# One layer of gated linear attention and an expert-choice FFN on one core: another order of the head's loads, stores, sums, transposes and gather

## What is computed

```
q, k = silu(xn Wq'), silu(xn Wk');  v = xn Wv';  log_f = log_sigmoid(xn Wf' + delta)
lf = cumsum(log_f) inside chunks of 128 tokens, 16 heads of 16 features
o  = (q exp(lf)) S  +  (q k' * exp(lf_i - lf_j), i >= j) v
S  = exp(tot) S + (k exp(tot - lf))' v                       # from chunk to chunk
s  = (o * rsqrt(mean(o*o)) * norm_weight) Wo'

affinity = softmax(xn gate_w');  per expert (8) the 128 tokens of each batch with the highest affinity
out[idx] += gating * ((silu(xi w_gate') * (xi w_up')) w_down')
x + s * silu(out)
```

## Time and profile before

| | us |
|---|---|
| median of 3 runs | 902.36 |
| lowest and highest | 902.20 and 903.24 |
| the profiled execution | 906.21 |
| its span in the trace | 904.5 |

### The profile page before, as it was taken

One profiled execution on the slowest core, in us unless ns is written; L12 is line 12 of the kernel. 1 busy time (PEld: TensorE's weight loads), 2 busy tenths in 40 slices (PEclk: granted clock), 3 DMA queues, 4 the chain that ended last, 5 costly groups with the idle time before them and its releaser, 6 DMA issues.

```text
span 904.5 us, 15830 instructions
## 1 busy us (share of the span) xinstructions
PE 799.0 (88%) x5648; PEld 681.6 (75%) x5648; DVE 570.1 (63%) x1034; ACT 498.4 (55%) x1165; POOL 427.5 (47%) x383
## 2 busy tenths in 40 slices
PE   1654389999999999999999999999999999999930
PEld 1443378888888888888888888888888888888820
DVE  5676256556755676557655775567656755656585
ACT  4653565566546664566556655765566545653421
POOL 5645561357426662556165815563356425561120
PEclk9965699999999999999999999999999999999965
DMA  8829798776766685769587777776776757754827
GB/s 280 283 102 196 181 256 296 170 165 146 219 145 164 159 214 148 161 158 199 168 190 167 141 226 155 173 158 189 172 147 180 199 145 210 167 111 160 248 80 223
DMA packets 132847, 163.89 MB, mean 181 GB/s; under 512 B 11808, under 2 KB 102432, under 8 KB 132640
## 3 DMA queue, kind: packets, MB, share of 16 engines
q1 hardware_dynamic: 119904, 145.00, 58.1%
q0 software_dynamic: 12288, 16.79, 11.9%
q10 hardware_dynamic: 576, 1.09, 0.3%
HBM read 117.48 MB, written 45.35 MB: 180 GB/s over the span
## 4 chain that ended last, share of the span: by engine, by line
PE 72%; DVE 7%; DMA 5%; ACT 3%; issue 3%; POOL 3%; SPq 1%; DVEq 0%; ACTq 0%; POOLq 0%
PE g_ps L1415 17%; PE up_ps L1415 16%; PE y_ps L1441 16%; PE m_ps L1333 5%; PE a_ps L1381 4%; PE o_ps L1405 4%; PE m_ps L1341 3%; PE m_ps L1363 2%; DMA w_raw<-w_experts 2%; PE m_ps L1358 1%; POOL w_r L794 1%; PE o_ps L1397 1%; ACT dec_both L963 1%; DVE sg L1284 1%; DMA w_r<-ffn_dram 1%
## 5 line engine op out<-in xcount | busy, mean ns | idle before, releaser
L1441 PE MATMUL y_ps<-w_r,hid_r 128*128 128x256 f32 x1536 | 206.2, 284 | 5.2 <-DVE hid_r L1298 5.2
L1415 PE MATMUL up_ps<-xgt,w_r 128*128 128x512 f32 x768 | 204.8, 402 | 0.0
L1415 PE MATMUL g_ps<-xgt,w_r 128*128 128x512 f32 x768 | 202.0, 398 | 2.5 <-DVE sg L1284 2.5
L1441 PEld LDWEIGHTS y_ps<-w_r,hid_r 128*128 128x128 f32 x1536 | 194.2, 191 | 6.4 <-DVE hid_r L1298 5.6
L1284 DVE SCALAR_TENSOR_TENSOR sg<-sg,g_ps 128x512 f32<-128x512 f32 x128 | 87.5, 684 | 166.6 <-ACT sg L1054 166.6
L794 POOL TENSOR_TENSOR w_r<-w_raw,w_r 128x768 fp32r<-128x768 f32 x64 | 122.2, 1909 | 95.5 <-ACT w_r L983 95.3
L1415 PEld LDWEIGHTS up_ps<-xgt,w_r 128*128 128x128 f32 x768 | 139.2, 190 | 25.9
L1415 PEld LDWEIGHTS g_ps<-xgt,w_r 128*128 128x128 f32 x768 | 135.6, 189 | 25.9 <-DVE sg L1284 2.9
L1054 ACT ACTIVATE sg<-g_ps 128x512 f32<-128x512 f32 x128 | 76.4, 597 | 124.1 <-PE g_ps L1415 124.1
L824 POOL DMA_INDIRECT ffn_dram<-y_sb,idx_all x64 | 103.2, 1612 | 83.6 <-DVE y_sb L1206 67.9
L789 POOL TENSOR_SCALAR_AFFINE_SELECT lb_row<-lb_row 128x1024 f32<-128x1024 f32 x64 | 78.1, 1230 | 104.6 <-DMA lb_row<-lb_tiles 104.5
(11 more groups left out here) (239 smaller groups left out, 944.4 us busy)
## 6 DMA issues: line engine op xcount, KB each, us to landing
lb_row<-lb_tiles SPq DMA_DIRECT2D x64, 512.0 KB, 4.7
w_raw<-w_experts SPq DMA_DIRECT2D x64, 384.0 KB, 3.6
qk_dram<-qk_r SPq DMA_DIRECT2D x32, 512.0 KB, 4.3
k_st<-qk_dram SPq DMA_DIRECT2D x96, 128.0 KB, 4.2
arena<-qk_dram SPq DMA_DIRECT2D x192, 64.0 KB, 4.3
x_all<-x SPq DMA_DIRECT2D x8, 512.0 KB, 10.3
xn_dram<-xn SPq DMA_DIRECT2D x8, 512.0 KB, 4.8
e_row<-lb_tiles SPq DMA_DIRECT2D x64, 64.0 KB
```

The costliest lines, as they stand in the source:

```text
L1415: mm = pe.matmul(bank[:, :], w_r[:, m, a, at:at + P], xgt[:, b, k, half * 512:(half + 1) * 512], start=(j == 0 and k == 0), stop=(j == len ...
L1441: mm = pe.matmul(y_ps[:, j, :], hid_r[p][:, a, j * P:(j + 1) * P], w_r[:, m, b, DOWN:DOWN + D], start=(m == 0 and q == 0 and j % 2 == 0), ...
```

## The change

Nothing is computed in another way. Instructions are put in another place in the order, and the second gate chain gets other tiles:

- **TensorE:** the affinities are turned after the first job in place of the third; `sums_turned(0)` goes ahead of job v; `sums(1)` goes from ahead of job "top" to behind it.
- **ScalarE:** Ln of the first gate part goes behind the fourth job's Tanh, with the third job's high part ahead of it; the fourth job's high part goes ahead of `sums(0)`; job v's copy goes behind `gates_left(0)`.
- **GpSimd:** low part 2 goes ahead of `gates_log(0)`; the first gather goes ahead of `gates_left(1)`, and waits for one store of the block before (xt_stored) in place of the second chain's end.
- **VectorE:** (TOP_STEPS takes the place of 3 * ROUNDS in every wait on topk) the last replacement of the search is left out; nothing read its result.
- **SyncE:** the keys of the first stack are loaded once the key stores have landed (`load_keys`), both query stores go ahead of `store_lb(0)`, and the first stack's queries ahead of `load_lb`. In the loop `load_rows` goes from step 2 of a batch's 16 to step 6.
- **Tiles:** `spare[1]` uses y_sb, th and small, and xg no longer.

```diff
@@ tiles
-                 [t[:, n:n + 384] for n in (0, 384) for t in (y_sb[:, :, :].rearrange("p t d -> p (t d)"),
-                                                              xg[:, :, :].rearrange("p t d -> p (t d)"))]]
+                 [y_sb[:, 0:2, :].rearrange("p t d -> p (t d)")[:, 0:384], th[:, 0:384],
+                  y_sb[:, 2:4, :].rearrange("p t d -> p (t d)")[:, 0:384], small[:, 512:896]]]
@@ SyncE
+                def load_keys(ch):
+                    b, s, cols = ch // TPB, ch % 2, slice(ch % TPB * P, (ch % TPB + 1) * P)
+                    for g in range(3):
+                        rows = qk_dram[b % 2, K, K_PART[g], :, cols].rearrange("(r p) n -> p r n", p=PAIR)
+                        sp.dma_start(f32(k_st[s][PAIR * g:PAIR * (g + 1), :, :]), rows).then_inc(st_in[s], 16)
                 def load_stacks(ch):
...
+                    if ch >= 1:
+                        load_keys(ch)
                     for g in range(3):
-                        rows = qk_dram[b % 2, K, K_PART[g], :, cols].rearrange("(r p) n -> p r n", p=PAIR)
-                        sp.dma_start(f32(k_st[s][PAIR * g:PAIR * (g + 1), :, :]), rows).then_inc(st_in[s], 16)
...
                 for i in range(2):
                     store_part(0, i)
-                store_lb(0)
+                for n in range(2):
+                    sp.wait_ge(qk_out[n], 16)
+                load_keys(0)
                 for i in range(2, 4):
                     store_part(0, i)
+                store_lb(0)
+                load_stacks(0)
                 sp.wait_ge(d_out, 16)
                 sp.wait_ge(chain, CHAIN)
                 for n in range(2):
                     load_lb(n)
-                load_stacks(0)
                 load_rows(0)
                 load_stacks(1)
...
-                    if at == 2 and b + 1 < B:
-                        if b >= 1:
-                            load_x(b + 1)
+                    if at == 2 and b >= 1 and b + 1 < B:
+                        load_x(b + 1)
+                    if at == 6 and b + 1 < B:
                         load_rows(b + 1)
@@ GpSimd
+    TOP_STEPS = 3 * ROUNDS - 1
...
                 def gather(e, half):
-                    pool.wait_ge(topk, 3 * ROUNDS + 2)
+                    pool.wait_ge(topk, TOP_STEPS + 2)
                     if e == 0 and half == 0:
-                        pool.wait_ge(chain, 2 * CHAIN)
+                        pool.wait_ge(xt_stored[0], 16)
...
                 low_part(1)
+                low_part(2)
                 gates_log(0)
-                low_part(2)
...
                     if u == 0:
+                        gather(0, 0)
                         gates_left(1)
-                    if u == 1:
-                        gather(0, 0)
@@ ScalarE
                 evacuate(FIRST[2])
-                gates_ln(0)
                 split(FIRST[2])
                 evacuate(FIRST[3])
+                gates_ln(0)
+                split(FIRST[3])
                 sums(0)
-                split(FIRST[3])
                 sums_turned(0)
+                gates_left(0)
                 evacuate(FIRST[4])
-                gates_left(0)
@@ TensorE
-                for job in FIRST[:3]:
-                    make(job)
+                make(FIRST[0])
                 pe.wait_ge(soft, 5)
                 for c in range(2):
                     mm = pe.transpose(aff_ps[:, c * P:(c + 1) * P], kd[:, c * P:(c + 1) * P], ident[:, :])
                 mm.then_inc(aff_turned, 1)
-                make(FIRST[3])
+                for job in FIRST[1:4]:
+                    make(job)
                 sums(0)
+                sums_turned(0)
                 make(FIRST[4])
-                sums_turned(0)
...
-                    if u == 0:
-                        sums(1)
                     if u == 1:
                         sums_turned(1)
                     if 1 <= n <= XS:
                         down(n - 1)
                     if second:
                         make(second)
+                    if u == 0:
+                        sums(1)
```

More of the change, by code:

```diff
@@ L836, in gates_sum @@
                     if p == 1:
-                        pool.wait_ge(xt_stored[0], 16)
+                        pool.wait_ge(xt_stored[1], 16)
                     shape = [P, PART[p].stop - PART[p].start, H]
@@ L957, in decays @@
                     if t == 3:
-                        act.wait_ge(topk, 3 * ROUNDS + 1)
+                        act.wait_ge(topk, TOP_STEPS + 1)
                     if t >= 4:
@@ L1201, in gated @@
                         dve.wait_ge(zeroed, 16 * B)
-                        dve.wait_ge(topk, 3 * ROUNDS + 2)
+                        dve.wait_ge(topk, TOP_STEPS + 2)
                     dve.wait_ge(scattered, 16 * TPB * n)
@@ L1245, in search @@
                 def search(first, rounds):
-                    for n in range(3 * first, 3 * (first + rounds)):
+                    for n in range(3 * first, min(3 * (first + rounds), TOP_STEPS)):
                         top_step(dve, topk, n, aff_t, top_val, top_at)
@@ L1271, in _ @@
                     evacuate(job)
-                dve.wait_ge(topk, 3 * ROUNDS)
+                dve.wait_ge(topk, TOP_STEPS)
                 low, high = slice(0, B * E), slice(B * E, 2 * B * E)
@@ L1367, in make @@
                     elif kind == "top":
-                        pe.wait_ge(topk, 3 * ROUNDS + 1)
+                        pe.wait_ge(topk, TOP_STEPS + 1)
                         pe.transpose(m_ps[:, 0:P], top_rev[:, :], ident[:, :])
```

## The result

The change is faster: 896.95 us (median of four runs, 895.99 to 897.55) against 902.70 us for the kernel before on the same chip. The ratio is 0.9942, with a 95% interval of 0.9922 to 0.9962, that is 3.4 to 7.0 us. The medians differ by 5.75 us, where 8.0 was forecast. The predicted 894.4 is 2.6 us too low; the range of 890.0 to 899.5 holds the time. The profiled execution of the change took 896.94 us, its own median, with a span of 895.2 us. That of the kernel before was 3.5 us above its median, so the two profiles differ by 9.3 us and the medians by 5.75. In the second set of runs one execution of the change (1164 us) and one of the kernel before (1042 us) ran at a lower clock, and the ratios leave them out.

What follows compares the result with a forecast made beforehand. The head was taken to bound the gain, set by three weight loads in a row and SyncE's queue. Terms 4.5 + 3.3 + 1.5 - 1.3 = 8.0 us took the median from 902.36 to 894.4; range 890 to 899.5.

Steps and rivals of the forecast that it cites:

- rival (d): Solid stretch: moved row loads make weight loads land 2.6 us late six times; net +7.6, time 910; chance 0.06.
- Rival (a): Head: query stores land in 4.3 us, so queries are late; gain 5.2, time 897.2; chance 0.12.
- Rival (b): Head's end: moved row loads block weight blocks 6 and 7, landing after 11.0 us; time 897.9; chance 0.13.
- (c): Head: weight blocks 2 and 4 land in 3.5 us instead of 5.3; gain 11, time 891.4; chance 0.15.
- part 4: SyncE's moved row loads: weights leave at 92.05, 7.85 us earlier; block 7 taken at 120.1, 8.0 us earlier.
- Part 1: Prologue's early sums, stores and keys: search some 4 us earlier, lb_row no gain, second chain still ends at 76.5.
- Part 2: TensorE's second sums start at 76.7 (3.4 us earlier), top transposes leave the path (1.1 us): job v 4.5 us earlier.
- Part 3: GpSimd's first gather goes at about 78 instead of 87.13, costed at nothing.
- that cover: GpSimd's last gates step, behind the gather's 5 us, ends near 84, needed only after 86; losing this slack costs up to 2 us.
- The term for landings: Head's weight loads: blocks 2 and 4 land in 5.3 us instead of 6.82 (1.5 us gained); block 6 takes 6.82.
- 3.3 + 1.5 - 1.3 = 3.5: Moved row loads: 3.3 us of SyncE queue order, 1.5 of shorter landing, less 1.3 for rows ahead of block 6.
- The 4.5 for the prologue and the gather: Head up to job v: sums 3.4 us earlier plus 1.1 for the top transposes, with the gather costed at nothing.

Runs made afterwards that it cites:

- the second set of runs: The changed kernel unaltered, run again with a second profile, against the kernel before: ratio 0.9947 (0.9927 to 0.9967).
- both repaired: The change with mask(1) held until VectorE's four copies are through and the first gather back in step 1: 895.03 us, ratio 0.9923 to the kernel before.

## Why the prediction was right, and where it was off

**The start and the end of the head.** That only the head moves was right: the solid stretch is unchanged (687.54 busy of 690 against 687.60), which refutes rival (d). Block 7 was forecast at 120.1 and came at 120.73 and 119.27. Rival (a) didn't come: TensorE waited 1.6 us for the queries, long before it had the search's result. By the time alone 896.95 can't be told from that rival's 897.2; only the marks in the profile part them. Rival (b) would have block 7 at 121.5 and more; (c) had it at 117.1.

**The step that was off: the profiled execution carried over to the median.** The prediction took 8.0 us from the one profiled execution and set the result 3.85 below it, as if that excess lay outside the head. In the second profile of before most of it is gone, and it had lain in the head: 4.5 us of span are missing, 3.55 of these already at block 7, 1.2 by the earlier sums and most of the rest by the landings of the weights. From that profile's 124.57 to the forecast 120.1 are 4.5 us, and to the measured 119.27 to 120.73 they are 3.8 to 5.3; the medians differ by 5.75 and, in the second set of runs, by 4.8 (902.34 times 0.0053). The forecast place was good, partly by luck (part 4), and the place that it was subtracted from was a late one. The forecast span of 896.5 was within 1.5 us of both profiles of the change (895.2 and 895.0).

**Part 1** was nearly right in its marks: affinities at 47.99 (forecast 48.0), the copies at 73.97 (74.5), first lb_row issued at 66.03 (66.9). mask 0 came at 71.25, not 72.5, so its transfer wasn't the fixed end that the prediction made of it (by its own sign part 1 was wrong there), and the second chain ended at 75.66, 0.8 us before the forecast 76.5.

**Part 2** was mis-sized. The sums start at 77.77, not 76.7, and job v at 81.81, not 80.8. The chain was through at 75.66; the slow copies, 2.1 us over the 0.87 us of before, held kd, which frees m_ps, and with it the top transposes that now stand ahead of the sums. With the last copy at its old price the sums start at 76.74 (both repaired). Here an edit put VectorE's copies beside GpSimd's work which in the kernel before they followed. The prediction moved the copies at their old price.

The Trainium skill, page "SBUF — State Buffer", section "SBUF: two separate sides", tells that VectorE and GpSimd share a pair of ports under an exclusive lock: whichever of certain VectorE instructions and GpSimd's starts first holds it for the whole instruction, and the other is blocked. The rows agree: a copy of 0.22 us takes up to 1.14 and ends with GpSimd's instruction. By this rule the term could have been foreseen.

**Part 3**, the gather costed at nothing, with "If that cover went, up to 2 us", was half right. Of 4.4 to 5.9 us of wait at tot_t 0 to 2.2 reached TensorE, and moving it back gained no time that the runs can tell. But block 0 came at 91.24 or 90.96, against 89.3 for its shifted place (93.76 less 4.5), so the first later weight load left at 93.99, not 92.05: 2 us late. In this profile 1.07 of it is the later start of the sums and the rest, 0.9, is from here; in the second profile the sums start at 78.32 and block 0 follows 12.64 us later, against a forecast 12.6, so all of it is from the sums.

**Part 4** had two errors that cancel. The load that left 1.9 us late landed in at most 3.0 us (issued 93.99, used 97.00) in place of the 5.3 taken, and block 2 was used at 97.00, forecast 97.4. The term for landings was too long there, and right later: block 6 was used at 115.75, forecast landed at 116. Of the terms of the sum, 3.3 + 1.5 - 1.3 = 3.5 stood for the rows and the landing behind them, and the runs put them at 2.0 and 2.5. The 4.5 for the prologue and the gather measured 2.4 to 2.8. Both came out below their terms although block 7 came where it was forecast; the sum had started from a late profile.

## What to carry to other kernels

Before a difference is read off one profile, ask for a second one of the same kernel: here two of them differ by 4.5 us, 3.55 of it in the first 125, nearly as much as the change brings. When short VectorE copies are moved, look at what GpSimd runs beside them at the new place, and put GpSimd's movable work behind them. And a wait that a moved transfer frees is worth only as much as the next queue lets through: here 2.3 us at block 7 turned into 3.2 us more of waiting behind a store.

## What the runs showed of the hardware

A VectorE copy or cast of 64x128 float32 between tiles in SBUF took 0.21 to 0.22 us alone and 0.57 to 1.14 us when GpSimd was already in an instruction, ending each time within 0.1 us of that instruction's end. A copy that had started 0.08 us ahead of GpSimd's instruction took 0.21. The search's instructions beside GpSimd's work weren't slowed in the change; the same replacement took 0.41 us with GpSimd busy (67.99) as without (78.26 in the kernel before).

Four indirect transfers issued by GpSimd beside TensorE's sums went with waits of 4.4 to 5.9 us in ScalarE and, in the profile of the change, 6.3 in VectorE, which the profile puts to "remote"; four plain transfers from the same queue at the same time did not. In step 1 the same gather had no such wait before tot_t, but in two of seven profiles VectorE waited 2.1 us, until 0.7 to 0.8 us after the gather's last instruction. The mechanism wasn't found.
